# A graph-convolution kernel: routed groups in two 64-row strips, loops over groups of 512 edges, and four tables for the indexed adds

## What is computed

```python
h = x @ W_in2f
Wij = ssp(f_ij @ W_filt1 + b_filt1) @ W_filt2 + b_filt2      # ssp(v) = softplus(v) - log 2
Wij = Wij * rcut_ij[:, None]
x_ij = h[idx_j] * Wij                                          # idx_j = dst
agg = jax.ops.segment_sum(x_ij, idx_i, num_segments=n_atoms)   # idx_i = src
out = ssp(agg @ W_out1 + b_out1) @ W_out2 + b_out2
result = layernorm(x + out)
```

## Time and profile before

| | |
|---|---|
| median of three executions | 2651.81 us (2647.66 to 2652.65) |
| the profiled execution | 2648.1 us, span of its instructions 2646.3 us |
| mean granted TensorE clock | 0.963 of full speed |
| TensorE matmuls busy | 2360.8 us (89% of the span) |
| TensorE weight loads | 1665.8 us, beside matmuls |
| GpSimd busy | 1906.8 us (72%) |
| VectorE busy | 1684.8 us (64%) |
| ScalarE busy | 1597.0 us (60%) |
| first scatter starts, last scatter starts | 102.51 us, 2526.32 us |

### The profile page before, as it was taken

How to read it: one execution, slowest core, us unless ns; L and a number is a source line. 1 busy time by engine, 2 the same in 40 slices (tenths; PEclk the granted TensorE clock), 3 DMA queues, 4 the chain that set the end, 5 groups by cost and what they waited for, 6 DMA issues and landing times.

```text
span 2646.3 us, 59597 instructions
## 1 busy us (share of the span) xinstructions
PE 2360.8 (89%) x16274; PEld 1665.8 (63%) x16274; DVE 1684.8 (64%) x3700; ACT 1597.0 (60%) x3509; POOL 1906.8 (72%) x1208
## 2 busy tenths in 40 slices
PE   3678999899899999899898999999898999999978
PEld 3456666666666666666666666666666666666645
DVE  6466666566666666666665666666676666666637
ACT  1466666666665656656566656656566656656503
POOL 1378877777777777777777777777777777767821
PEclk8599999999999999999999999999999999999989
DMA  7566655556565655665565556555555555556524
GB/s 272 147 130 94 90 92 88 85 87 87 81 91 79 90 86 84 90 85 84 86 89 79 89 82 89 90 79 90 90 86 80 91 80 89 92 77 89 68 70 135
DMA packets 356079, 248.75 MB, mean 94 GB/s; under 512 B 89739, under 2 KB 329846, under 8 KB 355514
## 3 DMA queue, kind: packets, MB, share of 16 engines
q0 software_dynamic: 169200, 77.08, 30.5%
q1 hardware_dynamic: 181362, 153.75, 25.2%
q10 hardware_dynamic: 5148, 13.49, 1.3%
HBM read 148.41 MB, written 95.76 MB: 92 GB/s over the span
## 4 chain that ended last, share of the span: by engine, by line
PE 38%; DMA 25%; issue 16%; POOL 10%; ACT 6%; DVE 3%; POOLq 1%; ACTq 0%; SPq 0%; DVEq 0%
DMA table<-total,index 24%; PE unit_psum L1398 15%; POOL table L640 10%; PE unit_psum L1384 6%; PE both_psum L1345 5%; PE pre_psum L1335 4%; PE total_psum L1359 3%; PE both_psum L1369 2%; ACT soft L753 1%; ACT h_dst L775 1%; ACT soft L751 1%; PE both_psum L1341 1%; ACT ring L797 1%; PE pre_psum L1497 1%; DMA x_t<-in_x_t 0%
## 5 line engine op out<-in xcount | busy, mean ns | idle before, releaser
L640 POOL DMA_INDIRECT table<-total,index x1175 | 1878.9, 1599 | 628.3 <-issue 281.3
L1398 PE MATMUL unit_psum<-scat_hot,ring 128*128 128x348 bf16 x5238 | 833.7, 317 | 13.1 <-DVE scat_hot L1137 13.0
L775 ACT ACTIVATE h_dst<-both_psum,cols 128x128 f32<-128x128 f32 x1564 | 445.2, 369 | 500.9 <-PE both_psum L1369 471.5
L1398 PEld LDWEIGHTS unit_psum<-scat_hot,ring 128*128 128x128 bf16 x5238 | 512.5, 99 | 276.6 <-issue 13.5
L1384 PE MATMUL unit_psum<-moving,route_hot 128*128 128x386 bf16 x2328 | 434.0, 328 | 133.5 <-ACT ring L797 115.0
L1066 DVE SCALAR_TENSOR_TENSOR hidden<-pre_psum,soft 128x1024 f32<-128x1024 f32 x196 | 239.9, 1224 | 389.8 <-ACT soft L755 329.4
L1345 PEld LDWEIGHTS both_psum<-w_f,hidden 128*128 128x128 f32 x3128 | 420.8, 195 | 33.1 <-issue 0.2
L1345 PE MATMUL both_psum<-w_f,hidden 128*128 128x128 f32 x3128 | 422.3, 279 | 0.0
L1384 PEld LDWEIGHTS unit_psum<-moving,route_hot 128*128 128x128 bf16 x2328 | 211.5, 98 | 270.9 <-ACT ring L797 130.9
L760 ACT ACTIVATE total<-total_psum 128x516 f32<-128x516 f32 x294 | 178.2, 606 | 308.8 <-DMA table<-total,index 226.3
L1147 DVE TENSOR_TENSOR acc_t<-acc_t,unit_psum 128x348 f32<-128x348 f32 x306 | 157.4, 514 | 255.7 <-PE unit_psum L1398 235.5
(11 more groups left out here) (115 smaller groups left out, 1672.3 us busy)
## 6 DMA issues: line engine op xcount, KB each, us to landing
dst_b<-dst SPq DMA_DIRECT2D x391, 128.0 KB
src_b<-src SPq DMA_DIRECT2D x295, 128.0 KB, 6.4
f_t<-in_f_t SPq DMA_DIRECT2D x98, 256.0 KB
table<-total,index POOLq DMA_INDIRECT x1175
window<-h_parts SPq DMA_DIRECT2D x391, 32.0 KB
table<-zeros ACTq DMA_DIRECT2D x15, 640.0 KB, 4.4
parts<-table SPq DMA_DIRECT2D x36, 256.0 KB, 3.2
h_parts<-h_out SPq DMA_DIRECT2D x12, 384.0 KB, 4.0
```

What stands on the lines that cost most here:

```text
L640: pool.indirect_dma_start(tables[table], bass.IndirectOffsetOnAxis(index[:, i, k:k + 1], 0), total[:, i, k, 0:DIM], None, compute_op=ALU.a ...
L775: last = act.activation(h_dst[:, b, d], source, ACT.Copy, scale=cols[:, q[1] % COL_BUFFERS, weight:weight + 1])
L1398: last = pe.matmul(unit_psum[:, unit_bank(q, c), 0:SLICE], ring[:, r % RING, b, part * DIM:(part + 1) * DIM], scat_hot[:, r % RING, c * SL ...
```

## The change

- The number of routed groups becomes 7 in each unit of 24 (places 3, 6, 10, 13, 17, 20, 23), 112 in all instead of 97; the last unit's 7 groups (384 to 390) are all plain. So 279 groups are plain instead of 294, with 1,115 scatters instead of 1,175.
- Slots: 7 slot tiles (instead of 6) of 128 rows, each cut in two strips of 64 rows. A strip is a bucket of 448 nodes, 14 buckets cover 6,272 nodes. A bucket holds at most 64 edges of a tile position instead of 128. The ring has 7 entries; one slot tile is added up per routed group: 2 strips x 7 groups x 3 parts = 42 matmuls of 448 columns over 64 rows, the strips by turns, strip 0 to one bank of unit_psum and strip 1 to the other. They are issued in two bursts, the older five groups (30) and the newest two (12). One one-hot of 448 columns serves both strips.
- route has 7 tiles x 4 matmuls, route_hot 896 columns instead of 768.
- All engines step by groups instead of quads; two units are written out, a loop runs 14 times over 24 groups, then 7 groups and the leftovers. soften is three calls placed in two steps. message and same have three buffers instead of two. The leftover slices are issued between groups 388 and 391.
- Four tables instead of three (zeroed, loaded and added in the last layers; the transpose of the fourth is another matmul per tile).
- Chunks of tables, x and out are laid out with rows 512 bytes each, `(t p)` instead of `(p t)`, so that acc_t is read without a step.

```diff
-UNROLL = 6
-FIRST = 2 * UNROLL
-LOOPS = (QUADS - 2 - FIRST) // UNROLL
-TABLES = 3
+UNIT = 24
+ROUTED_AT = (3, 6, 10, 13, 17, 20, 23)
...
+TABLES = 4
...
-BUCKETS, SLICES, SLICE = 6, 3, 348
-BUCKET = SLICES * SLICE
-SLOT_ROWS = BUCKETS * P
+STRIPS = 2
+STRIP = P // STRIPS
+SLOT_TILES = 7
+BUCKETS = STRIPS * SLOT_TILES
+BUCKET = 448
+SLOT_ROWS = SLOT_TILES * P
...
                 for k in range(TABLES):
                     sp.dma_start(parts[:, b, k, 0:tiles * DIM].rearrange("p (t d) -> p t d", d=DIM),
                                  tables[k][bass.ds(chunk_number(c) * CHUNK, tiles * P), :]
-                                 .rearrange("(p t) d -> p t d", t=tiles)).then_inc(parts_loaded[b], 16)
+                                 .rearrange("(t p) d -> p t d", t=tiles)).then_inc(parts_loaded[b], 16)
...
                 if not isinstance(c[0], int):
-                    zero(1 + b, c[0])
+                    for k in range(1 + b, TABLES, 2):
+                        zero(k, c[0])
...
+            def add_up(m, k, groups, part):
+
+                for r in part:
+                    pe.wait_ge(hot_done, through_hots(m, len(groups) - 1 - groups.index(r)))
+                    for p in range(3):
+                        first, final = r == groups[0] and p == 0, r == groups[-1] and p == 2
+                        for strip in range(STRIPS):
+                            rows = slice(strip * STRIP, (strip + 1) * STRIP)
+                            last = pe.matmul(unit_psum[:, strip, 0:BUCKET],
+                                             ring[rows, r % RING, k, p * DIM:(p + 1) * DIM],
+                                             scat_hot[rows, r % RING, :], start=first, stop=final)
+                if groups[-1] in part:
+                    last.then_inc(slice_mm_done, 1)
+
+            def add_slices(m, begin):
+
+                groups = routed_for(m)
+                part = groups[0:-2] if begin else groups[-2:]
...
+            def step_narrow(g):
+                m, j, groups = interval(g)
+                routing = j >= 0 and routes(plus(m, -1))
+                if exists(g):
+                    second_layer(g)
+                if j == 1:
+                    add_slices(m, False)
+                if routing and groups == 3 and j == 2:
+                    route(m, 2)
+                if routing and groups == 4 and j == 2:
+                    route(m, 0)
+                if routing and groups == 4 and j == 3:
+                    route(m, 4)
+                if g[1] % 2 == 0 and exists(plus(g, 2)):
+                    first_layer(pair_of(plus(g, 2)))
...
+                if j == 0:
+                    add_slices(m, True)
...
+                if m[1] == ROUTES and j >= 4:
+                    for e in range(2 * (j - 4), min(2 * (j - 4) + 2, SLOT_TILES)):
+                        last_slices(e)
...
                         pe.matmul(both_psum[:, b, d], half_sum[:, b, d], ident[:, :], start=True, stop=False)
-                        last = pe.matmul(both_psum[:, b, d], parts[:, b, 2, d], ident[:, :], start=False, stop=True)
+                        for table in range(2, TABLES):
+                            last = pe.matmul(both_psum[:, b, d], parts[:, b, table, d], ident[:, :], start=False,
+                                             stop=(table == TABLES - 1))
```

More of the change, by code:

```diff
@@ L110, in table_of, with number, plus, routed @@
-def table_of(q, tile, n):
-    return (n * TILES * q[1] + tile) % TABLES
-def adds_before(q, tile, k, n):
-    s = n * TILES * q[1] + tile
-    return 16 * UNROLL * n * TILES // TABLES * q[0] + 16 * ((s - k + TABLES - 1) // TABLES)
+def number(g):
+    return UNIT * g[0] + g[1]
+def plus(g, n):
+    return g[0], g[1] + n
+def routed(i):
+    return 0 <= i < LAST_UNIT and i % UNIT in ROUTED_AT
+def plain(i):
+    return i >= 0 and not routed(i)
+def every(i):
+    return i >= 0
+def through(g, kind=every):
+    return sum(map(kind, range(UNIT))) * g[0] + sum(map(kind, range(g[1] + 1)))
@@ new lines, in last_before, with exists, is_at, pair_of @@
+def last_before(g, kind, n=0):
+    for i in range(g[1] - 1, -1, -1):
+        if kind(i) and (n == 0 or (g[1] - i) % n == 0):
+            return g[0], i
+    return None
+def exists(g):
+    return not isinstance(g[0], int) or 0 <= g[1] < GROUPS
+def is_at(g, n):
+    return isinstance(g[0], int) and g[1] == n
+def pair_of(g):
+    return g[0], g[1] // 2
+def through_pair(pair):
+    return UNIT // 2 * pair[0] + (pair[1] + 1)
+def quad_landed(quad):
+    return 16 * (UNIT // QUAD // 2) * quad[0] + 16 * (quad[1] // 2 + 1)
@@ new lines, in quad_number, with through_half, table_adds, unit_adds @@
+def quad_number(quad):
+    return UNIT // QUAD * quad[0] + quad[1]
+def through_half(g):
+    return 2 * g[0] + g[1] // HALF + 1
+def table_adds(k, adds):
+    return (adds - k + TABLES - 1) // TABLES
+def unit_adds(g, kind, tile):
+    return TILES * sum(kind(i) for i in range(g[1] // UNIT * UNIT, g[1])) + tile
+def table_of(g, kind, tile):
+    return unit_adds(g, kind, tile) % TABLES
+def adds_before(g, kind, tile, k):
+    per_unit = table_adds(k, TILES * sum(map(kind, range(UNIT))))
+    return 16 * per_unit * g[0] + 16 * (g[1] // UNIT * per_unit + table_adds(k, unit_adds(g, kind, tile)))
@@ L120, in routes, with tiles_in, interval @@
+def tiles_in(g):
+    if isinstance(g[0], int):
+        return max(0, min(TILES, REAL_TILES - g[1] * TILES))
+    return TILES
+def interval(g):
+    i = g[1]
+    if i < 0:
+        return (g[0], 0), -1, 0
+    if i >= LAST_UNIT:
+        return (g[0], ROUTES), i - LAST_UNIT, 4
+    m = sum(map(routed, range(i)))
+    start = max([k for k in range(i) if routed(k)], default=-1) + 1
+    return (g[0], m), i - start, min(k for k in range(i, i + UNIT) if routed(k)) - start + 1
 def routes(r):
     return not isinstance(r[0], int) or 0 <= r[1] < ROUTES
[L125 to L127 removed]
@@ L1466, in _, with step_general @@
+            def step_general(g):
+                if exists(g):
+                    second_layer(g)
+                if exists(plus(g, -1)):
+                    sum_repeated(plus(g, -1), every)
+                if g[1] % 2 == 0 and exists(plus(g, 2)):
+                    first_layer(pair_of(plus(g, 2)))
             with pe.If(is_narrow):
-                run_quads(pe, step_narrow)
-                last_slices()
-                pe.wait_ge(acc_done, after_slice((0, QUADS + BUCKETS - 1), SLICES - 1))
```

1204 lines of the change are left out of this document (575 added, 629 removed).

## The result

The changed kernel takes **2888.02 us** (median of 4; 2882.2 to 2907.43) against 2652.23 us (4 executions of the kernel before on the same chip): a ratio of 1.0904 with a 95% interval of 1.0849 to 1.0959, so 9% slower where I forecast 7% faster. The profiled execution took 2884.5 us, span 2882.4.

A forecast was written before the change was run, and what follows sets the result against it. TensorE was taken to bound the loop, with GpSimd near its limit. From 2648.1 us, loop -207, last groups +10, head +14 and +9, tail -23 and +26 gave 2477 us, range 2428 to 2530, 64%.

The forecast's parts named there:

- the allowance for waits: Loop: TensorE's waits in a unit of 24 groups, taken as 7 us, bounds 0 and 17.
- Rival B: Loop: ScalarE, in strict order at 102 us, holds ring banks; unit about 144 us, 2591 us in all; 12%.
- A: Loop: TensorE and ScalarE wait only where GpSimd does; unit 131 us, 2379 us in all; 13%.
- C: Loop: the two strips' slice matmuls don't overlap; TensorE's unit 162 us, 2891 us in all; 8%.
- D: Whole kernel: waits and tail together just cancel the gain; 2648 us; 3%.
- TensorE's work: Loop: TensorE's counted work of a turn or unit falls from 132.6 to 123.0 us.
- Slices: Loop: a routed group's 42 slice matmuls, strips overlapping, take 4.35 us; bounds 3.99 and 7.98.
- Head: Before the loop: place_routed's longer chain costs +14 us and zeroing a fourth table +9.
- -23: Tail: with leftover slices issued under the last scatters, first parts are ready about 12 us behind the last scatter instead of 35.
- +26: Last layers: 512-byte packets at 48 ns make a chunk's transfers 7.7 us against TensorE's 5.5, over 12 chunks.
- The table's wait: Loop: with four tables GpSimd's wait for a table, 10.3 us a turn, should go; it buys little alone.
- -207 + 10: Loop: turns of 137 instead of 149.7 us save 207 us; the seven last, all plain groups cost 10.

The follow-up runs named there:

- e12: Changed kernel with hidden, seventh ring copy, gather and route one-hots earlier, first split later, other ring copies before the ln: 2495.8 us, 0.941 of the kernel before.
- e14: e12 with VectorE's finish_hidden moved back to the end of odd steps, as in the changed kernel: 2873.4 us, 1.082 of the kernel before.
- e2: Changed kernel with ScalarE copying the seventh slot tile to the ring before the ln instead of behind it: 2870.0 us, 1.081 of the kernel before.
- e4: Changed kernel with each burst of slice matmuls running all of strip 0, then all of strip 1: 3465.2 us, 1.307 of the kernel before.
- e5: Changed kernel with three tables instead of four: 2881.0 us, 1.088 of the kernel before.
- e6: Kernel before with four tables instead of three and nothing else of the change: 2663.1 us, 1.004 of the kernel before.
- e13: e12 with three tables instead of four: 2495.1 us, 0.938 of the kernel before.
- e1: Changed kernel with VectorE calling finish_hidden right behind the messages in odd steps: 2787.3 us, 1.049 of the kernel before.

## Why the prediction was wrong

**The step that failed is the allowance for waits: "I take 1 us for each routed group, 7 a unit".** A turn was predicted at 123.0 + 6.8 + 7 = 137 us and took 164.0, so 27 us a turn, 440 us in all, are missing there. Measured as the sum has it, all that a turn takes beyond 123.0 + 6.8 is 34.2 us, where I had 7. With nothing changed but orders (e12) the same instructions run in 140.0, near the 137 of the sum. Of the 24.1 us a turn between after and e12, 19.5 are TensorE standing and 4.6 the same matmuls at the lower clock level (mean granted clock 0.95 for 0.97). I had bounded the term at 17 from the old kernel's 1.7 us of waits a quad, that is, from a different order (nor does the working give 17: 1.7 for each of seven intervals is 12, twice that is 24). How far the old order loses time says nothing of a new one. What I had in hand was the diff with the new step lists, and reading them as a cycle (what does VectorE's finish_hidden stand behind, and what does that wait for?) would have pointed at it, though not at its size: even with that chain in mind I expected turns of 152 to 160 us of e14, which took 163.3. The one wait that I looked at, the ring's, was the smaller of the two.

**Rival B, order stalls,** had the right mechanism with the wrong size: 144 us a unit for 164, and it named ScalarE's ring, not VectorE's hidden. e2 shows that the ring alone is worth 18 us, e14 that with hidden late all other orders together bring 15. A (GpSimd's floor) never came near: GpSimd waits 312 us for an index in 8.5 turns. C fell: 4.18 us of slices a routed group (2.94 us for 30, 1.24 for the other 12), not 7.98. That its 2891 us lie 3 us from the measured 2888 is chance; e4, where the strips do go one after the other, takes 577 us more. D was no case.

**TensorE's work.** Slices 4.35 us predicted, 4.18 measured; the drain of the array on a change of tiling (the Trainium skill, TensorEngine Tiling (Array Packing), Key Properties) is no more than the 0.2 us by which 42 matmuls exceed 21 x 0.190. The measured 5.7/2.94 = 1.9 for two strips stands against the share of 0.77 that I drew from the Trainium skill, TensorE: Matmul & The Clock Gate, Measured speedup vs the span model, for four tiles; the share here is 0.97, and the row decided rightly. The work falls by 2.2 us a turn by the busy times (138.0 to 135.8), 6.8 with the clock restored (131.2), against 9.6 by my count (132.6 to 123.0).

**Head: +23 predicted, +24 measured, by luck.** The first scatter starts at 126.57 us for 102.51. With three tables (e5) it starts at 121.84, so the fourth table costs 4.7 us of the 24, where I had 9, and the rest of the change 19.4, where I had 14:

```profile
126.57 1.73 POOL L686 DMA_INDIRECT table<-total,index  x1 [99.64 <-DVE index L1176]
```

**Tail: -23 held, +26 did not.** The last scatter and the start and pace of the last layers (timelines of GpSimd and TensorE, answering to the earlier trace rows):

```profile
2782.33 1.54 POOL L686 DMA_INDIRECT table<-total,index  x1 [0.31 <-issue]
```

```profile
2796.25 0.77 PE L1546 MATMUL both_psum<-ident,half_sum 128*128 128x128 f32 x2 [17.10 <-POOL half_sum L726]
...
2816.81 1.02 PE L1556 MATMUL pre_psum<-acc_t,w_o 128*128 128x512 f32 x2
...
2822.32 1.02 PE L1556 MATMUL pre_psum<-acc_t,w_o 128*128 128x512 f32 x2
```

TensorE starts 12.4 us behind the last scatter's end (12 predicted, 35 before), and the chunks are 5.51 us apart, TensorE's own work, where I had 7.7. What fed that number was the packet of 512 bytes at 48 ns. The DMA queues from 2800 to 2882, answering to the earlier trace rows:

```profile
q1 hardware_dynamic: 21696, 10.75, 44.7%
q10 hardware_dynamic: 6444, 3.20, 13.1%
```

44.7% of 16 x 82 us over 21,696 packets is 27 ns each, of 495 bytes on average, and both queues together hold the engines 58% busy. The line through two averages of mixed packets was wrong. 495 bytes in 27 ns are 18 bytes a ns, and the 1,700 bytes in 90 ns of the tail before are 19: here the time went by the bytes alone, which was my lower bound. Only the loop's 759 bytes in 57 ns were slower; those are other transfers, and no run shows why. The Trainium skill, DMA: Bandwidth & Descriptors, Specifications, which I had set aside for those rows, puts line rate at 512 bytes and more; this trace agrees in so far as these rows moved as many bytes a ns as the longer ones before. From last scatter to end the tail takes 98.5 us, before 118.4.

**The table's wait** went as forecast (an add waits 31.5 us for its table in the whole run), and that it buys little alone, too: e5, e6 and e13 show that it buys nothing.

**Together.** The profiled execution missed the forecast by 2884.5 - 2477 = 407 us. From the first scatter to the last it takes 2655.8 us for 2423.8, so +232 where I had -207 + 10: 429 us, which are the 440 of the turns less the 10 for seven plain groups at the end, of which nothing is left (14.3 x 16.3 is 233 already). The head adds 1, and the tail, -20 for +3, takes 23 off. And from e12: the sum with 140.0 for 137 and without the +26 is 2477 + 49 - 26 = 2500, and e12 takes 2495.8. Its 3 us a turn beyond the sum are not waits: TensorE stands 8.8 us, as little as 137 us leave beside the work (138.0 - 9.6 = 128.4 us busy), but is busy 131.2. So with the orders mended the allowance of 7 us was right, and the work came out 2.8 us a turn too small.

## What to carry to other kernels

When a change brings a new order of issue, don't carry the old order's waits over: for each engine's list, ask of every instruction that TensorE needs next what stands ahead of it and what that one waits for. If the walk comes back to TensorE within the step, it can pay part of that loop nearly every time (in e14 in 67 of 77 such steps), with VectorE and ScalarE busy no more than 60%. Mend such waits together and measure them together: one alone (the ring) gave 18 us of the 116 that it was worth beside the other, since the matmuls stayed at the lower clock and a part of the time went to the next wait, and a good change can look bad until the last is gone.

## What the runs showed of the hardware

- Two bfloat16 matmuls of 448 columns on the two 64-row halves of the array take 0.196 us as a pair (30 in 2.94 us), 1.9 times as fast as by the rate of one over 128 rows; one strip after the other 30 took 5.04 us at a granted clock of 1.00 and 8.13 at one of 0.61.
- Where TensorE stood up to 2.9 us at a time in many steps (after, e1, e2, e14), the same matmuls took 136 to 137 us of a turn at a mean granted clock of 0.93 to 0.95 in the loop, where e12 has 131.2 at 0.97: a long wait was paid again in the work behind it, as L1402 shows with 1.78 us at a granted clock of 0.54 for 1.05 at 1.00.
- Packets of 495 bytes on average, nearly all 512-byte rows of the tables, took 27 ns on an engine, 18 bytes a ns, where those of 1,700 bytes in the kernel before took 90 ns, 19 bytes a ns.
